# More staging homes, three weight pairs rounded by GpSimd, two product buffers, and prefix sums of the second batch without a carried row

## What is computed

```
x = x + attn(layernorm(x)):
    q, kv = x @ W_q.T, x @ W_kv.T                 # 16 heads of 32
    qf, kvf = fft(q), fft(kv), each / its norm    # per head
    values = ifft(qf * cumsum(kvf, over tokens)).real
    attn = values @ W_o.T
x = x + ffn(layernorm(x)):
    wq = w.astype(float8_e4m3fn).astype(float32)  # gate, up (512 x 1536), down (1536 x 512)
    ffn = ((silu(x@gate * gs) * (x@up * us)) @ down) * ds
```

## Time and profile before

| | |
|---|---|
| Median of 3 runs | 483.61 us |
| The profiled execution | 482.7 us |
| Its span (first to last instruction) | 480.6 us |
| PE busy | 437.8 us, 91% |
| DVE busy | 295.4 us, 61% |
| ACT busy | 185.8 us, 39% |
| POOL busy | 110.7 us, 23% |
| DMA | 26.13 MB, 54 GB/s over the span |
| granted PE clock, mean | 0.978 |

### The profile page before, as it was taken

One profiled execution on the slowest core, in us unless ns is written; L12 is line 12 of the kernel. 1 busy time (PEld: TensorE's weight loads), 2 busy tenths in 40 slices (PEclk: granted clock), 3 DMA queues, 4 the chain that ended last, 5 costly groups with the idle time before them and its releaser, 6 DMA issues.

```text
span 480.6 us, 5431 instructions
## 1 busy us (share of the span) xinstructions
PE 437.8 (91%) x1976; PEld 283.9 (59%) x1976; DVE 295.4 (61%) x491; ACT 185.8 (39%) x298; POOL 110.7 (23%) x105
## 2 busy tenths in 40 slices
PE   4996968599768789999998999999999999999995
PEld 4883546286335446668654656677755676555554
DVE  6988799447898858633586547343685536432224
ACT  4856313435443234433352425233534234222220
POOL 0203760000035742012016541040044400300002
PEclk9999898899989979999999999999999999999999
DMA  8921031131222030006000000013000000110002
GB/s 263 390 97 44 0 110 66 45 87 44 89 87 87 4 129 1 1 1 220 0 2 0 22 24 1 2 69 107 0 0 2 0 2 0 45 44 2 0 0 87
DMA packets 14522, 26.13 MB, mean 54 GB/s; under 512 B 1824, under 2 KB 2080, under 8 KB 14496
## 3 DMA queue, kind: packets, MB, share of 16 engines
q1 hardware_dynamic: 14208, 25.77, 15.9%
q10 hardware_dynamic: 288, 0.02, 0.0%
HBM read 21.57 MB, written 4.19 MB: 54 GB/s over the span
## 4 chain that ended last, share of the span: by engine, by line
PE 71%; DVE 12%; POOL 7%; issue 4%; ACT 3%; DMA 2%; SPq 0%; DVEq 0%; POOLq 0%; ACTq 0%
PE bg L364 15%; PE bu L364 15%; PE bd L380 14%; PE ba L289 14%; PE ba L323 6%; PE bd L289 2%; POOL qk L1011 2%; POOL qk L1010 2%; DVE hT L705 2%; PE ba L332 2%; POOL ks L1001 1%; DVE qk L765 1%; PE bg L289 1%; POOL qk L999 1%; PE ba L302 1%
## 5 line engine op out<-in xcount | busy, mean ns | idle before, releaser
L380 PE MATMUL bd<-dw,fu 128*128 128x512 f32 x376 | 99.8, 408 | 0.0
L364 PE MATMUL bg<-hT,gu 128*128 128x512 f16 x384 | 94.1, 390 | 5.9 <-ACT sl L549 4.9
L364 PE MATMUL bu<-hT,gu 128*128 128x512 f16 x384 | 91.5, 382 | 2.7 <-DVE ff L832 2.7
L380 PEld LDWEIGHTS bd<-dw,fu 128*128 128x128 f32 x376 | 70.3, 191 | 15.6 <-DVE fu L837 0.4
L832 DVE SCALAR_TENSOR_TENSOR ff<-bu,us,sl 128x512 f32<-128x512 f32 x48 | 35.9, 748 | 68.5 <-PE bu L364 61.1
L289 PE MATMUL ba<-wf,xTs 128*128 128x512 f32 x288 | 69.1, 396 | 0.2 <-DVE wf L697 0.2
L364 PEld LDWEIGHTS bg<-hT,gu 128*128 128x128 f16 x384 | 35.4, 100 | 54.2 <-issue 11.6
L364 PEld LDWEIGHTS bu<-hT,gu 128*128 128x128 f16 x384 | 37.6, 98 | 49.5 <-DVE ff L832 3.7
L289 PEld LDWEIGHTS ba<-wf,xTs 128*128 128x128 f32 x288 | 54.0, 188 | 12.3 <-DVE wf L697 0.3
L549 ACT ACTIVATE sl<-bg,gs 128x512 f32<-128x512 f32 x48 | 33.0, 686 | 58.1 <-PE bg L364 57.9
L1001 POOL TENSOR_TENSOR ks<-qk,ks 128x512 f16<-128x512 f32 x16 | 19.0, 1193 | 137.1 <-ACT ks L510 137.1
(11 more groups left out here) (164 smaller groups left out, 500.3 us busy)
## 6 DMA issues: line engine op xcount, KB each, us to landing
h<-x_dram SPq DMA_DIRECT2D x16, 256.0 KB, 4.8
out_dram<-h SPq DMA_DIRECT2D x16, 256.0 KB, 2.0
hT<-gate_w_dram SPq DMA_DIRECT2D x6, 512.0 KB, 4.4
xTr<-xT_dram SPq DMA_DIRECT2D x12, 256.0 KB, 4.4
hT<-down_w_dram SPq DMA_DIRECT2D x6, 512.0 KB, 4.6
hT<-up_w_dram SPq DMA_DIRECT2D x4, 512.0 KB, 3.7
hT<-w_q_dram SPq DMA_DIRECT2D x4, 256.0 KB, 4.1
gu<-w_kv_dram SPq DMA_DIRECT2D x4, 256.0 KB, 5.3
```

The lines of the kernel that those rows point to most:

```text
L364: m = e.matmul(bk[:, :], gu[:, c, 4 * w + k, col:col + P], hT[:, b % 2, part, k, :], start=k == 0 and part == 0, stop=k == KT - 1 and part ...
L380: m = e.matmul(bd[t][:, :], fu_at(n)[:, part, P * t:P * t + P], dw[:, i, :], start=i == 0 and part == 0, stop=i == NI - 1 and part == 1)
```

## The change

- `STAGE` names homes: `n0` (hT[:,0], which holds the raw W_q until its fold is done), `n1` (the old `stage`), `x1` (h[:,1]), `ff`, and `g2` (where W_o was). The homes of pairs 0, 1, 4, 8 and 9 are new. Every pair gets a DMA semaphore of its own.
- Pairs 0, 1 and 4 are rounded by GpSimd with three instructions each (`pool_round`), ahead of its first `pool_ks`. DVE's roundings 0, 1 and 4 go; pair 5 moves from before the loop into step 0, and the others are reordered.
- In batch 0 product 1 has its own buffer (`tu`), is issued straight after product 0, and the products wait for the one two before. Product 0 also waits for the rounding of pair 4.
- In batch 1 the prefix sum multiplies all tiles before (12 more matmuls), the carried rows, their three DMAs and additions go, and `ks` of its tiles 1 to 3 are made together at i = 3 and 4.
- The first two `act_x`/`pool_x` of batch 1 come before the W_o copies and the last two after them; `act_size` of pair 3 comes later.

```
-STAGE = [0, 1, 2, 3] + [0, 1] * 7
-SIZES = {1: (8, 10), 2: (10, 11), 3: (11, 13), 4: (13, 14), 5: (14, 15), 6: (15, 16), 7: (16, 18)}
-ROUNDS = {0: (6, 8), 1: (8, 9), 2: (9, 11), 3: (11, 12), 4: (12, 13), 5: (13, 14), 6: (14, 16), 7: (16, 17), 8: (17, 18)}
   (pairs first to end - 1)
+STAGE = (("n0", 0), ("n0", 1), ("x1", 0), ("x1", 1), ("ff", 0), ("n1", 0), ("n1", 1), ("n1", 0), ("g2", 0), ("g2", 1),
+         ("n1", 1), ("n1", 1), ("n1", 0), ("n1", 1), ("n1", 0), ("n1", 0), ("n1", 1), ("n1", 0))
+POOL_ROUNDED = (0, 1, 4)
+ROUNDED = (2, 3, 5, 6, 8, 9, 7, 10, 12, 13, 14, 11, 15, 16, 17)
+LOADS = {1: (7, 10), 2: (12, 13), 3: (14,), 5: (11,), 6: (15, 16), 7: (17,)}
+SIZES = {1: (7, 10), 2: (12,), 4: (13,), 5: (14,), 6: (11,), 7: (15, 16), 8: (17,)}
+ROUNDS = {0: (5, 6), 1: (8, 9, 7), 2: (10, 12), 5: (13,), 6: (14, 11), 7: (15,), 8: (16,), 9: (17,)}
   (pairs one by one)
...
-        T_OWN = [False, False, True, False] + [True] * 12
+        T_OWN = [False, True, False, True] + [True] * 12
...
-            tiles = range(t + 1) if b == 0 else (t,)
+            tiles = range(t + 1) if b < 2 else (t,)
...
-            act_size(e, 6)
-            act_size(e, 7)
+            act_size(e, 8, 9)
             for b in range(NB):
...
-            dve_round(e, 0, 1)
...
-            dve_round(e, 1, 2)
+            dve_round(e, 2)
...
             dve_product(e, 0, 0)
+            dve_product(e, 0, 1)
             dve_scale(e, 0, 2, 0)
             dve_scale(e, 0, 3, 0)
-            dve_product(e, 0, 1)
-            dve_round(e, 2, 3)
             dve_pT(e, 0, 0)
             dve_product(e, 0, 2)
             dve_pT(e, 0, 1)
             dve_product(e, 0, 3)
-            dve_round(e, 3, 4)
+            dve_round(e, 3)
             dve_pT(e, 0, 2)
             dve_o(e, 0, 0)
-            dve_round(e, 4, 5)
             dve_pT(e, 0, 3)
...
-            dve_round(e, 5, 6)
...
+        def pool_round(e, n):
+            unit = size_at(n)
+            e.wait_ge(*sized(n))
+            e.tensor_scalar(unit, unit, UNIT, None, ALU.max).then_inc(p_unit, 1)
+            e.wait_ge(p_unit, rounded(n)[1])
+            e.tensor_tensor(stage_at(n), stage_at(n), unit, ALU.add).then_inc(p_add, 1)
+            e.wait_ge(p_add, rounded(n)[1])
+            e.tensor_tensor(pairs[n][1], unit, stage_at(n), ALU.subtract).then_inc(p_rd, 1)
...
             pool_x(e, 0, 1)
+            for n in POOL_ROUNDED:
+                pool_round(e, n)
             pool_ks(e, 0, 0)
             pool_ks(e, 0, 1)
+            pool_x(e, 1, 0)
+            pool_x(e, 1, 1)
+            pool_ks(e, 0, 2)
             pool_product(e, 0, 0)
-            pool_ks(e, 0, 2)
             pool_ks(e, 0, 3)
...
-            sp_weights(e, 0, 2)
+            sp_weights(e, 0, 1)
             e.dma_start(cst2, cst2_d).then_inc(d_cst2, 16)
+            sp_weights(e, 4)
             sp_x(e, 0)
-            sp_weights(e, 2, 4)
+            sp_weights(e, 2, 3)
...
-            sp_weights(e, 4, 6)
+            sp_weights(e, 5, 6)
+            sp_weights(e, 8, 9)
             sp_xT(e, 1, 2)
             sp_xT(e, 1, 3)
-            sp_weights(e, 6, 7)
             sp_x(e, 1)
-            sp_weights(e, 7, 8)
```

More of the change, by code:

```diff
@@ L559, in act_fu, with act_size @@
             e.activation(fu_at(n)[:, 0, :], ff[:, n % 2, :], ACT.Copy).then_inc(a_fu, 1)
[L561 to L570, removed]
+        def act_size(e, *ns):
+            for n in ns:
+                e.wait_ge(d_w[n], 16)
+                if n == 6:
+                    e.wait_ge(s_fold, 8)
+                if n == 12:
+                    e.wait_ge(*rounded(8))
+                    e.wait_ge(*rounded(9))
+                if n % 6 > 3 and n > 5:
+                    e.wait_ge(*rounded(n - 6))
+                e.activation(size_at(n), stage_at(n), ACT.Abs, scale=2.0 ** 20).then_inc(a_size, 1)
         def scalar_program(e):
@@ L584, in scalar_program @@
             act_qk(e, 0, 0, 1)
+            act_size(e, 4)
             e.wait_ge(d_cst, 16)
@@ L606, in scalar_program @@
             act_ks(e, 0, 3)
+            act_size(e, 3)
             for j in range(KT):
@@ L646, in scalar_program @@
                             act_ks(e, nxt, 0)
+                        if i == 4 and nxt == 1:
+                            for t in range(1, NT):
+                                act_ks(e, nxt, t)
                         if i == 4:
@@ L667, in scalar_program @@
                     if b == 0 and i in SIZES:
-                        for pair in range(*SIZES[i]):
-                            act_size(e, pair)
+                        act_size(e, *SIZES[i])
                     if b + 2 < NB and 6 <= i < 10:
@@ L698, in dve_wf, with dve_round @@
                             ALU.subtract).then_inc(v_wf, 1)
-        def dve_round(e, first, end):
-            for n in range(first, end):
-                e.wait_ge(a_size, n + 1)
+        def dve_round(e, *ns):
+            for n in ns:
+                e.wait_ge(*sized(n))
                 e.scalar_tensor_tensor(out=stage_at(n), in0=size_at(n), scalar=UNIT, in1=stage_at(n), op0=ALU.max,
                                        op1=ALU.add).then_inc(v_add, 1)
-                e.wait_ge(v_add, n + 1)
+                e.wait_ge(v_add, rounded(n)[1])
                 e.scalar_tensor_tensor(out=pairs[n][1], in0=size_at(n), scalar=UNIT, in1=stage_at(n), op0=ALU.max,
@@ L775, in dve_product @@
             e.wait_ge(v_qn, n + 1)
-            if b > 0 and t < NT - 1:
-                e.wait_ge(a_row, 3 * (b - 1) + t + 1)
-            if n:
+            if b > 1 and t < NT - 1:
+                e.wait_ge(a_row, 3 * (b - 2) + t + 1)
+            if b > 0:
                 e.wait_ge(p_z, n)
+            elif t > 1:
+                e.wait_ge(p_z, t - 1)
+            elif t == 0:
+                e.wait_ge(*rounded(4))
             if own:
@@ L1031, in gpsimd_program @@
             pool_product(e, 0, 3)
-            for k in range(KT):
-                pool_x(e, 1, k)
+            pool_x(e, 1, 2)
+            pool_x(e, 1, 3)
             for b in range(NB):
@@ L1041, in gpsimd_program @@
                             pool_ks(e, nxt, 0)
+                            if nxt == 1:
+                                for t in range(1, NT):
+                                    pool_ks(e, nxt, t)
                         if i == 4:
@@ L1073, in sp_x, with sp_weights @@
                 e.dma_start(h[:, b % 2, t, :], x[D * b + P * t:D * b + P * t + P, :]).then_inc(d_x[b % 2][t], 16)
-        def sp_weights(e, first, end):
-            for n in range(first, end):
+        def sp_weights(e, *ns):
+            for n in ns:
                 before = stage_before(n)
```

68 lines of the change are left out of this document (37 added, 31 removed).

## The result

The change makes the kernel slower: 487.22 us, the median of 4 runs (486.33 to 487.43), against 483.59 for the kernel before (4 runs, 483.45 to 483.87), a ratio of 1.0071 [1.0053, 1.0088]. The same kernel, run again later as a control on another chip, gave 485.54 us, 1.0052 [1.0033, 1.0071]. The forecast was 480.6 us, faster than before. The profiled execution took 487.21 us with a span of 485.4 us, so it has to be explained why the span grew by 4.8 us; the control's span was 482.1 us, 1.5 more than before. That execution was the quickest of the control's six (483.94 us, their median 485.54), and the profiled one of before was 0.9 us under its median, so neither span difference is the difference of the medians.

What follows compares the result with a forecast made beforehand. From 40 to 182 us DVE, GpSimd and ACT passing tiles on were the bound, DVE busiest. Terms -5.3 + 0.0 + 2.3 = -3.0 took 482.7 to 479.7, plus 0.9 to the median: 480.6 us; range 473 to 488.

Steps and rivals of the forecast that it cites:

- GpSimd 6.1 us a pair: Start-up: GpSimd rounds pairs 0, 1 and 4 at 6.1 us each with handoffs, 18.3 us for three.
- rival B: Norm of tiles 0 and 1: long GpSimd roundings, deciding from 7.1 us a pair, cost +5.5, 489 us; chance 0.15.
- Rival A: Start-up: port turns cost little, the norm is not late, -8.7 us in all, 475 us; chance 0.20.
- 51.0: Start-up: GpSimd's first product comes at 51.0 us instead of 44.33, 6.7 us late.
- The half clock of 90 us goes, 1.3 more: After the first silu: PE's gap shrinks and the half clock of 90 to 95 us goes, gaining 1.3 us.
- DVE in the loop: Batch 0: DVE's gate-times-up at 131.5 instead of 128.2 (step 3), 143.7 against 146.5 (5), 163.2 against 165.5 (7).
- part 3: Loop up to step 8: second batch's prefix sums without the carry, net 0.0 us, bounds -3.5 and +3.
- gate starts at 171.1: Step 8: gate waits for pair 15, rounded behind product 3, and starts at 171.1 us instead of 170.8.
- Rounding 17, +2.3: Step 9: rounding 17 ahead of step 10's gate-times-up delays batch 1's hT; PE waits 2.3 us more, bounds +1.5 and +3.5.
- Batches 1 to 3: nothing: Rest of the kernel behind step 10's gate-times-up: 0 us of change.
- Rival D: Loop: second half-clocked window, DVE 1.5 us later at step 8, +3.5 in step 9; about +4.5, 485 us; chance 0.15.
- the forecast's -4.0: Start-up and first silu: DVE's gate-times-up of step 0, batch 0, starts 4.0 us earlier than in the kernel before.

Runs made afterwards that it cites:

- load first: The changed kernel with weight loads ahead of the transposed-x loads in SyncE's list at steps 4, 6 and 7: 484.01 us, 1.0013 of the kernel before.
- both orders mended: The changed kernel with weight loads queued ahead of x loads and rounding 17 in step 8 behind rounding 16: 481.23 us, 0.9961 of the kernel before.

## Why the prediction was wrong

It had the wrong sign; by its own steps:

1. *GpSimd 6.1 us a pair* (taken from between 5.0 and 8.9): 7.2 to 8.5, beyond rival B's threshold of 7.1. The mis-sized term is the one-input step, 2.77 instead of 1.3; the two-input step, 2.15, was within 0.2. B did not come true all the same; the step that was so much longer held no DVE instruction. Rival A's sign showed (L758 and L760 at 0.23 us) without A's time. The mechanism was half right: DVE and GpSimd did take turns, but at one small instruction and the rounding of pair 2, not at three of the norm's instructions, and the first product at 51.9 instead of 51.0 was in part luck. f(0) was -1.7 and -3.5 instead of -4.0. (The three ends are 0.2 us off in the working too: 18.1 + 18.3 is 36.4, not 36.6.)
2. *The half clock of 90 us goes, 1.3 more.* It went: up of step 1 started 1.74 us behind its gate instead of 3.03. But f(1) waits for a rounding and stands at -1.69, where f(0) did. PE's gain ended in a wait for DVE, and the sum counted it although its next term is again a wait for DVE.
3. *DVE in the loop.* Forecast for f(3), f(5), f(7), in times of before: +3.3, -2.8, -2.3; measured +1.6, -4.0, -3.1 (after). Following DVE's list was right to 1.7 us.
4. **The step that failed is part 3's "gate starts at 171.1" with its net of 0.0.** It followed DVE's list and asked when DVE would be free for pair 15; it never asked when pair 15 would be there. The load was issued at 162.38, 4.6 us after its home was free, and the row of ACT's magnitude names it. In times of before gate came at 173.3; with the load first it comes at 170.7 (the forecast's own terms give 170.9, not 171.1), and with both orders mended gate of step 9 is at -0.1 (the shift of f(0) taken off): the term would then have been right.
5. *Rounding 17, +2.3*: measured +2.4, twice; with it moved, the loss and the wait of L339 go. This step was right.
6. *Batches 1 to 3: nothing.* The profiled execution lost 0.6 us in each of two batches and the control none, by an order of turns (below). A cost of this kind was not in the sum, and no run separates it.

The forecast -3.0 and the measured +4.8 differ by 7.8 us: start-up 2.3, loop 4.2 (2.5 to 2.9 of it the load, 1.3 the clock), step 9 0.1, turns 1.2. For the control's +1.5 it is 0.5, 3.9, 0.1, 0. Rival D, 485 us by "a second half-clocked window and DVE later by 1.5 us at step 8", had the right place and nearly the size; its cause was another. The failed step doesn't explain all: with the load alone mended, which is the kernel that the forecast had in mind, the ratio is 1.0013 [0.9986, 1.004], no longer slower, but not the 0.994 of the forecast either. The rest is the start-up, the clock term and the turns. That the kernel with rounding 17 moved as well (0.9961, 481.2 us) lies near the forecast 480.6 is chance, since the forecast had already paid 2.3 us for rounding 17.

One more term was treated as fixed. Five profiles share this start-up, and their f(0) stand at -1.49 (both orders mended), -1.70 (after), -3.47 (control), -3.52 (load first) and -4.61 (rounding 17), so the forecast's -4.0 lies within the spread. It begins at the new home of pair 0: that home holds the raw W_q, and the load waits until PE has folded it. The load was issued at 13.78 us in after, 12.78 in the control and 11.61 with rounding 17 moved, ACT waited 1.73, 0.81 and 0 us for it, and GpSimd's first step began at 18.84, 17.77 and 17.23. The rest comes behind the first product: granted clock 0.50, 0.59 and 0.76 from 55 to 60 us, and 3.15, 2.49 and 1.90 us for the eight matmuls of the prefix sum of tile 3. The magnitude of pair 0, in after and then in the kernel with rounding 17 moved:

```profile
17.69 1.06 ACT L581 ACTIVATE gu<-hT 128x1024 bf16<-128x1024 f32 x1 [1.73 <-DMA hT<-gate_w_dram]
```

```profile
16.08 1.06 ACT L581 ACTIVATE gu<-hT 128x1024 bf16<-128x1024 f32 x1
```

In the kernel before, where pair 0 has a home of its own, this magnitude starts between 16.06 and 16.29 in the profiles of it and of four kernels with its start-up up to there (those run alone, and without carry and sizes together). Open is why the fold is slower in some executions: two of its last matmuls took 0.63 us in after and 0.39 with rounding 17 moved, at a granted clock given as 1.00 in both.

## What to carry to other kernels

When a list is rewritten, follow each tile, not each engine: for the rounding that a matmul waits for, the rows to look up are its last producer's, back to the DMA issue and to whatever stands ahead of that issue in its queue. A saving ahead of a wait or a half clock that stays may be worth nothing (the magnitudes behind the first silu: 1.4% on the kernel before, nothing on the change), so look first for the cheap cause of a large gap (here two magnitudes queued ahead of a silu) before adding buffers, homes or another engine. Parts that lose together may each gain alone, so price them one by one.

## What the runs showed of the hardware that was not expected

GpSimd's in-place one-input TENSOR_SCALAR on 1024 bf16 elements takes 2.77 us, more than its two-input TENSOR_TENSOR of as many elements, with float32 among them (2.15). DVE's two-input instructions of 0.23 us ran undisturbed beside it, three in each of five profiles, while beside TENSOR_TENSOR one took 2.05. The Trainium skill (SBUF — State Buffer, Who interferes with whom) names GpSimd reads without this exception; why this one is free, no run shows.

The order in which DVE and GpSimd take turns can flip between executions. Before, GpSimd's step went first (1.11 us) and DVE's three scales took 2.99; in the profile of after DVE's three took 1.89 and GpSimd's step, begun first, 2.92. The control showed the order of before (1.11 and 2.99). Timeline of before at 252 us, then of after at the same place:

```profile
252.11 1.11 POOL L1010 TENSOR_TENSOR qk<-tu 128x256 f32<-128x256 f32 x1 [4.96 <-DVE tu L786]
252.56 2.99 DVE L765 TENSOR_TENSOR qk<-qk,sc 128x512 f32<-128x512 f32 x3
```

```profile
255.73 2.92 POOL L1032 TENSOR_TENSOR qk<-tu 128x256 f32<-128x256 f32 x1 [4.95 <-DVE tu L802]
256.17 1.89 DVE L777 TENSOR_TENSOR qk<-qk,sc 128x512 f32<-128x512 f32 x3
```
